# Normalised x, gated activations and most weights held as 16-bit parts in place of fp32r in a transformer block

## What is computed

```python
x = x + attn_a(layernorm(x), Wq, bq, Wk, bk, Wv, bv, Wo, bo)
x = x + ffn(layernorm(x), w_gate, w_up, w_down)
x = x + attn_b(layernorm(x), Wqkv, Wout, bout)
x = x + ffn(layernorm(x), w_gate, w_up, w_down)

def ffn(x, w_gate, w_up, w_down):          # integers of -127 to 127, times 1/127
    gate, up = x @ wg.T, x @ wu.T          # 256 -> 768
    return (silu(gate) * up) @ wd.T        # 768 -> 256
```

## Time and profile before

| | |
|---|---|
| Median of 3 runs | 2221.99 us (2216.15 to 2224.67) |
| Span of the profiled execution, and its own time | 2225.3 us |
| PE busy, share of the span | 1928.7 us, 87% |
| PE weight loads | 1388.2 us, 62% |
| DVE | 1422.0 us, 64% |
| ACT | 1444.9 us, 65% |
| POOL | 796.1 us, 36% |
| Matmuls traced | 25221 |

### The profile page before, as it was taken

How to read it: one execution, slowest core, us unless ns; L and a number is a source line. 1 busy time by engine, 2 the same in 40 slices (tenths; PEclk the granted TensorE clock), 3 DMA queues, 4 the chain that set the end, 5 groups by cost and what they waited for, 6 DMA issues and landing times.

```text
span 2225.3 us, 63347 instructions
## 1 busy us (share of the span) xinstructions
PE 1928.7 (87%) x25221; PEld 1388.2 (62%) x25221; DVE 1422.0 (64%) x2971; ACT 1444.9 (65%) x3580; POOL 796.1 (36%) x1131
## 2 busy tenths in 40 slices
PE   5677889889898989989898998989899898989786
PEld 4463657666675766667576666757666675756545
DVE  5363667576676757667675765767576676765624
ACT  1227676676867677676767767676776867677580
POOL 0023243433424343442434344243434424344431
PEclk7788999999999999999999999999999999999886
DMA  7224344252435335243533424353342434333321
GB/s 190 72 44 97 62 111 100 78 107 81 106 68 126 85 84 108 77 106 64 126 85 87 105 82 100 67 126 85 86 106 76 111 70 120 81 95 86 73 61 35
DMA packets 129636, 201.87 MB, mean 91 GB/s; under 512 B 26768, under 2 KB 60560, under 8 KB 129312
## 3 DMA queue, kind: packets, MB, share of 16 engines
q1 hardware_dynamic: 129344, 197.80, 37.1%
HBM read 67.87 MB, written 51.52 MB: 54 GB/s over the span
## 4 chain that ended last, share of the span: by engine, by line
PE 55%; ACT 17%; DVE 10%; issue 5%; SPq 5%; DMA 4%; POOL 4%; ACTq 0%; POOLq 0%; DVEq 0%
PE gu_bank L1053 15%; PE d_bank L1069 7%; ACT s_bank L1167 7%; PE gu_bank L1081 7%; SPq L575 4%; PE s_bank L984 4%; PE s_bank L948 4%; ACT probs_B L1157 3%; PE gu_bank L1017 3%; PE s_bank L814 2%; PE gu_bank L1027 2%; PE s_bank L969 2%; PE s_bank L822 2%; ACT probs_A L1150 2%; PE gu_bank L1004 2%
## 5 line engine op out<-in xcount | busy, mean ns | idle before, releaser
L1167 ACT ACTIVATE s_bank<-s_bank 128x512 f32<-128x512 f32 x1024 | 602.9, 591 | 123.3 <-PE s_bank L948 123.0
L1576 POOL TENSOR_TENSOR h<-tmp,h 128x512 fp32r<-128x512 f32 x192 | 252.0, 1312 | 451.6 <-DVE h L1457 451.6
L1157 ACT ACTIVATE probs_B<-s_bank 128x512 f32<-128x512 f32 x640 | 334.5, 610 | 48.5 <-PE s_bank L969 45.8
L1053 PE MATMUL gu_bank<-xT,w_g 128*128 128x256 f32 x1536 | 235.5, 298 | 25.1 <-DVE tmp L1440 21.1
L1053 PE MATMUL gu_bank<-xT,w_u 128*128 128x256 f32 x1536 | 241.3, 298 | 4.2 <-DVE tmp L1440 1.6
L1196 ACT ACTIVATE tmp<-gu_bank 128x512 f32<-128x512 f32 x192 | 114.6, 597 | 196.1 <-PE gu_bank L1053 188.5
L1053 PEld LDWEIGHTS gu_bank<-xT,w_g 128*128 128x128 f32 x1536 | 208.6, 199 | 52.9 <-DVE tmp L1440 35.8
L1053 PEld LDWEIGHTS gu_bank<-xT,w_u 128*128 128x128 f32 x1536 | 208.0, 198 | 37.6 <-issue 20.4
L1440 DVE SCALAR_TENSOR_TENSOR tmp<-tmp,gu_bank 128x512 f32<-128x512 f32 x192 | 130.6, 681 | 152.5 <-ACT tmp L1196 151.0
L1069 PE MATMUL d_bank<-w_d,h 128*128 128x256 f32 x1536 | 224.8, 288 | 3.3 <-POOL h L1576 3.3
L948 PE MATMUL s_bank<-pack_b 48*128 48x512 f16 x1024 | 180.4, 394 | 43.5 <-DVE o_raw L1361 19.9
(11 more groups left out here) (140 smaller groups left out, 3303.5 us busy)
## 6 DMA issues: line engine op xcount, KB each, us to landing
pack_b<-src_b SPq DMA_DIRECT2D x768, 64.0 KB, 2.6
pack_a<-src_a SPq DMA_DIRECT2D x384, 64.0 KB, 2.3
x<-in_L_attn_a_x_dram SPq DMA_DIRECT2D x32, 512.0 KB, 4.9
o_scr_A<-o_raw SPq DMA_DIRECT2D x64, 256.0 KB, 2.4
o_scr_B<-o_raw SPq DMA_DIRECT2D x64, 256.0 KB, 2.4
xn<-o_scr_A SPq DMA_DIRECT2D x32, 256.0 KB
rden_on<-r_scr_A SPq DMA_DIRECT2D x32, 256.0 KB
x_scr<-x SPq DMA_DIRECT2D x16, 512.0 KB, 2.9
```

Of the source, the lines that this page charges most:

```text
L1053: last = pe.matmul(bank[:, f * D:(f + 1) * D], plain(w[:, k, c:c + P], exact), plain(given[:, k, half * D:(half + 1) * D], exact), start=k ...
L1157: act.activation(probs["B"][:, i, :], score_bank("NP", n // 2, q, n % 2)[:, :], ACT.Exp, scale=SM_SCALE)\
L1167: act.activation(bank[:, :], bank[:, :], ACT.Exp, scale=SM_SCALE, accum_out=den[:, 0, j, 2 * tile + e, t:t + 1]).then_inc(den_exp, 1)
L1576: pool.tensor_tensor(h[1][:, i % 2, :], tmp[:, i % 2, :], h[0][:, i % 2, :].bitcast(F32), ALU.subtract)\
```

## The change

1. `xT`, `wa_qk`, `wa_v`, `wb_qk`, `wb_v` and `h` become f16, high and low part; `w_g`, `w_u` and `w_d` become bf16, of which the first of three tiles holds the whole integer. `wa_o`, `wb_o` and the attention's output stay fp32r, the latter in two tiles of its own, `on_part`.
2. So that small low parts stay in f16's range, the weights of queries, keys and values are multiplied by `W_SCALE = 16` when they are split (and the biases of attention A once on DVE); exp takes `SM_SCALE / W_SCALE ** 2`, and `wa_o`, `wb_o` are divided by 16. The gated activations are multiplied by `h_scale` (a per-partition scalar from the largest weight) and the result by `h_back`.
3. At the start ACT copies each bank of integer weights twice (bf16 tile and fp32 staging), the three DMAs of L554 go, and POOL splits the staged weights into three bf16 parts by nine instructions of 128x1536 after `GM` of the first sequence. Only `program(False)` reads the second and third part. `EXACT` falls from 2048 to 256; the weights here are at most 127.

The counts of PE's instructions in `program(True)` are what they were. The core of the diff:

```diff
-        wa_qk = [sb(f"wa_qk{i}", [P, KT, 2 * D], F32R) for i in range(2)]
+        wa_qk = [sb(f"wa_qk{i}", [P, KT, 2 * D], F16) for i in range(2)]
...
-        w_g = sb("w_g", [P, KT, HID], F32R)
+        w_g = [sb(f"w_g{i}", [P, KT, HID], BF16) for i in range(W_PARTS)]
...
-        xT = [[sb(f"xT{b}{i}", [P, KT, S], F32R) for i in range(2)] for b in range(2)]
+        xT = [[sb(f"xT{b}{i}", [P, KT, S], F16) for i in range(2)] for b in range(2)]
...
-        on_parts = xT[0]
+        on_parts = [sb(f"on_part{i}", [P, KT, S], F32R) for i in range(2)]
...
-        h = [sb(f"h{i}", [P, 2, S], F32R) for i in range(2)]
+        h = [sb(f"h{i}", [P, 2, S], F16) for i in range(2)]
...
-            for n, (dst, a) in enumerate(((w_g, st_gT), (w_u, st_uT), (w_d, st_dT))):
-                sp.wait_ge(w_staged, (4, 8, 11)[n])
-                sp.dma_start(dst[:, :, :].bitcast(F32), a).then_inc(w_raw, 16)
...
+                        for n, w_part in enumerate(w[:1] if exact else w):
+                            last = pe.matmul(bank[:, f * D:(f + 1) * D], w_part[:, k, c:c + P],
+                                             given[:, k, half * D:(half + 1) * D],
...
+                act.activation(dst[0], given, ACT.Copy)
+                act.activation(dst[1], given, ACT.Copy).then_inc(w_staged, 1)
-            act.wait_ge(w_raw, 48)
...
+            then(dve.tensor_scalar(h_back[:, :], w_top1, W_LEAST, 2.0, ALU.max, ALU.mult))
+            then(dve.tensor_tensor(h_back[:, :], h_back[:, :], h_back[:, :], ALU.mult))
+            then(dve.reciprocal(h_scale[:, :], h_back[:, :]))
+            then(dve.tensor_scalar(h_back[:, :], h_back[:, :], 0.5 * DEQUANT ** 3, None, ALU.mult))
...
-                dve.tensor_tensor(t, t, gu_of("U", i, block, q)[:, :], ALU.mult).then_inc(gu_taken, 1)
+                dve.scalar_tensor_tensor(t, t, h_scale[:, 0:1], gu_of("U", i, block, q)[:, :], ALU.mult, ALU.mult).then_inc(gu_taken, 1)
...
-                dve.scalar_tensor_tensor(xs, tokens(d_bank), 0.5 * DEQUANT ** 3, xs, ALU.mult, ALU.add).then_inc(d_taken, 1)
+                dve.scalar_tensor_tensor(xs, tokens(d_bank), h_back[:, 0:1], xs, ALU.mult, ALU.add).then_inc(d_taken, 1)
...
+                    if q == 0:
+                        split_weights()
```

More of the change, by code:

```diff
@@ L411, in build @@
         wb_split = sem("wb_split")
-        w_raw = sem("w_raw")
+        w_parts = sem("w_parts")
+        b_scaled = sem("b_scaled")
+        w_spread = sem("w_spread")
         w_flag = sem("w_flag")
@@ L1047, in ffn_up @@
                     gu("GU"[up], i, block, q)
+                if not exact and part == 0 and i == 0 and FN[block, q] == 0:
+                    pe.wait_ge(w_parts, 3 * W_PARTS)
                 for k in range(KT):
@@ L1052, in ffn_up @@
                         c = (2 * pair + f) * P
-                        last = pe.matmul(bank[:, f * D:(f + 1) * D], plain(w[:, k, c:c + P], exact),
-                                         plain(given[:, k, half * D:(half + 1) * D], exact),
-                                         start=k == 0 and part == 0 and f == 0, stop=k == KT - 1 and part == 1, skip_group_check=True)
+                        for n, w_part in enumerate(w[:1] if exact else w):
+                            last = pe.matmul(bank[:, f * D:(f + 1) * D], w_part[:, k, c:c + P],
+                                             given[:, k, half * D:(half + 1) * D],
+                                             start=k == 0 and part == 0 and f == 0 and n == 0, stop=k == KT - 1 and part == 1,
+                                             skip_group_check=True)
                 if part:
@@ L1068, in ffn_down @@
                             c = f * D + t * P
-                            last = pe.matmul(bank[:, t, :], plain(h[part][:, i % 2, c:c + P], exact), plain(w_d[:, 2 * pair + f, :], exact),
-                                             start=pair == 0 and f == 0 and part == 0 and t == 0,
-                                             stop=pair == FT // 2 - 1 and f == 1 and part == 1, skip_group_check=True)
+                            for n, w_part in enumerate(w_d[:1] if exact else w_d):
+                                last = pe.matmul(bank[:, t, :], h[part][:, i % 2, c:c + P], w_part[:, 2 * pair + f, :],
+                                                 start=pair == 0 and f == 0 and part == 0 and t == 0 and n == 0,
+                                                 stop=pair == FT // 2 - 1 and f == 1 and part == 1, skip_group_check=True)
                 last.then_inc(d_ready if pair == FT // 2 - 1 else h_used, 1)
@@ L1265, in then, with split @@
                 dve.wait_ge(prep, done[0])
-            def split(parts, a):
-                then(dve.tensor_copy(parts[0], a))
-                return dve.tensor_tensor(parts[1], a, parts[0].bitcast(F32), ALU.subtract)
+            def split(parts, a, scale):
+                then(dve.tensor_scalar(parts[0], a, scale, None, ALU.mult))
+                high = parts[0].bitcast(F32) if scale < 1 else parts[0]
+                return dve.scalar_tensor_tensor(parts[1], a, scale, high, ALU.mult, ALU.subtract)
             def split_bank(n):
@@ L1275, in split_bank @@
                 w, c = ((wa_qk, 0), (wa_qk, D), (wa_v, 0), (wa_o, 0))[n]
-                split([a[:, :, c:c + D] for a in w], bank).then_inc(w_taken, 1)
+                split([a[:, :, c:c + D] for a in w], bank, W_SCALE if n < 3 else 1.0 / W_SCALE).then_inc(w_taken, 1)
             def to_float(n):
@@ L1609, in global_blocks, with split_weights @@
                     .then_inc(blocks_ready, 1)
+            def split_weights():
+                pool.wait_ge(w_staged, NBANKS - NSPLIT)
+                staged = (st_gT, st_uT, st_dT)
+                for n, (parts, rest) in enumerate(zip((w_g, w_u, w_d), staged)):
+                    pool.tensor_tensor(rest, rest, parts[0][:, :, :], ALU.subtract).then_inc(w_parts, 1)
+                    pool.wait_ge(w_parts, n * W_PARTS + 1)
+                    pool.tensor_copy(parts[1][:, :, :], rest).then_inc(w_parts, 1)
+                    pool.wait_ge(w_parts, n * W_PARTS + 2)
+                    pool.tensor_tensor(parts[2][:, :, :], rest, parts[1][:, :, :], ALU.subtract).then_inc(w_parts, 1)
             def global_maxima(q):
```

65 lines of the change are left out of this document (38 added, 27 removed).

## The result

The changed kernel takes 2150.1 us (median of four runs, 2146.4 to 2153.6) against 2219.1 us of the kernel before in the same series: a ratio of 0.9686, 95% interval 0.9665 to 0.9707. It is 69 us faster; 2168 were predicted, with a range of 2118 to 2207. The profiled execution of after has a span of 2151.9 us, 73.4 less than the 2225.3 of before. In the code after, L1053 has become L1057, L1069 L1075, L1081 L1087, L1004 L1008, L1017 L1021, L1027 L1031, L1446 L1466, L1457 L1477, L1462 L1482 and L1576 L1596.

The account below looks back on a forecast made before the run. PE was taken as the bound in most of a turn, ACT and DVE in a smaller part. From the profiled 2225.3 us, -61 + 3 + 4 = -54 gave 2171, then 2168 as the median is 3.3 lower; range 2118 to 2207.

Parts of the forecast that it names:

- Part 1: Matmul steps within groups on PE: f16 shortens them, saving 3.4 us (256 columns) and 1.0 us (512) a turn.
- Part 2: First matmul of PE groups whose weight load is exposed: 0.11 us falls to 0.01, taken as 2.0 us a turn.
- How much arrives: Share of PE's saving that reaches the end: 70%, 4.2 us a turn, 61 us over 14.6 turns.
- the first rival: ACT's exp and DVE's emptying of PSUM banks set the pace, a third of PE's gain arrives: 2198 us; chance 0.15.
- The clock: Rival: with PE in flight for less of each turn, further stretches fall to 1.2 GHz: 2243 us; chance 0.07.
- Theory C: Posed with the experiments: less time at the lower granted clock makes the gain, not the matmuls' steps; no chance given.
- DVE: Per-partition scalars add 1.0 us of DVE a turn, a sixth counts: 0.2 us a turn, 2 to 3 in all.
- The start: Second staging copies, tiny DVE instructions and POOL's split delay the start once: +4 us (2 to 9).
- The first 230 us and the end: First 230 and last 96 us: few sequences to interleave, then latency; no gain counted there.
- others take over: ACT and DVE limit once PE is quicker, a third of PE's gain arrives: 2198 us; chance 0.15.
- All arrives: Rival: every term at its upper bound and all on the path: 2120 us; chance 0.12.
- no quick load: Rival: weight loads stay at 0.11 us in bf16 beside f16, only costs remain: 2229 us; chance 0.06.

Follow-up runs that it names:

- rates: The kernel after with rows of 17 matmuls behind its last one; fp32r with 256 columns took 0.118 us a step with 128x128 and 128x32 weights, f16 0.109.
- The doses: First matmul of 24 gate and up groups a turn run two more times, in the kernel after (2201.5 us) and in the kernel before (2293.2 us).
- after_again: The kernel after, unchanged, run once more as a base on the same chip: 2152.6 us, ratio 0.9680 to before.
- before_pe_dose: The kernel before with the first matmul of 24 gate and up groups a turn run two more times: 2293.2 us, ratio 1.0325.
- pool_dose: The kernel after with a 128x4 memset before each of POOL's h_low steps, 12 times a turn: 2154.9 us, ratio 0.9709.
- out_f16: The kernel after with the output projections in f16 too and the factor 1/256 in the addition to x: 2145.0 us, ratio 0.9661.

## Why the prediction was right, and where it was not

**Part 1, steps within a group: size right, reason wrong.** 0.119 to 0.109 us and 0.236 to 0.215 were the forecast; the earlier trace rows and the rows of after give 0.119 to 0.109, and the starts in the trace 0.234 to 0.216 for 512 columns. The numbers came from rows of the same shapes, so they hold. The reason, "the two together come to 0.119", was wrong: `rates` keeps the step with a quarter of the weight columns. The 512-column row could have told: its streaming (0.213) hides a load of 0.11 entirely, and it had the larger excess (0.236).

**Part 2, first matmul of a group: right.** 0.11 us exposed for fp32r, 0.01 for f16: a fresh group of eight went from 1.22 to 1.05, of which 0.07 are its seven steps and 0.10 its start. Over all groups at the full clock, the first step of L1053 went from a mean of 0.170 to 0.114 us, of L1069 from 0.176 to 0.114, of L1004 from 0.187 to 0.112 and of L1081 from 0.286 to 0.224. For both parts together, take for each matmul at the full clock the time to the next start, or its own where none follows before it ends: the means went from 0.131 to 0.117 us (L1053), 0.133 to 0.117 (L1069), 0.132 to 0.117 (L1004) and 0.253 to 0.230 (L1081). That is 192 x 0.014 + 96 x 0.016 + 48 x 0.014 + 48 x 0.023 = 6.0 us a turn, where the sum had 6.4.

**How much arrives: right.** 70% was taken between 88% from the chain and the 35% of the first rival. The doses measured 0.79 and 0.58 at the two ends, 0.69 between, each uncertain by 0.08. 14.6 turns x 6.0 x 0.69 = 60 us, where 61 were predicted.

**The clock: the sign was missed.** It stood in the prediction as a risk only, and at the measured place it went the other way. The long stretch of steady turns, before and then after:

```profile
230.00:2000.00 1770.00, 1598.66 (x21708) 1154.05 (x21704) 1199.45 (x2520) 1227.45 (x3042) 676.90 (x952) 0.97 0.39 93
```

```profile
230.00:2000.00 1770.00, 1560.24 (x22195) 972.28 (x22193) 1241.44 (x2589) 1267.67 (x3172) 680.99 (x993) 0.98 0.38 96
```

The granted clock is 0.98 instead of 0.97 although PE is busy for less of the time. Summed from the trace's record of it, the time at the lower level in this stretch is 113 us before, 55 after and 61 in after_again; over the whole span 272, 190 and 217. More work on PE lowers it too: 79 in this stretch of before_pe_dose. Before, such stretches recur about each turn, at 1096.8, 1229.9 and 1356.2 us among others, the first one the four matmuls of 1.05 us in the earlier trace rows; between 1195 and 1800 us there are nine of them, none in after and three in after_again.

PE's time shows it as well. The four changed lines took 945 us before and 825 after, 120 less. Of these, 16 x 6.0 = 96 are steps at the full clock; the other 24 go with fewer of their matmuls at the lower level, 152 instead of 357. All other lines took 7.5 us more, which leaves the 112.7 less of PE's busy time.

What the clock is worth can be read from the runs, whose mean clock is on record: a run at a mean clock of 0.94 has 2 x 0.06 of its time at the lower level. The 25 runs of before beside the experiments have 0.944 on average, 250 us at the lower level, the nine of after 0.954, 199 us: 51 less, where the two traces have 82, since the traced run of before had one of the lower clocks (0.939). Among the 25 runs of one and the same kernel, the time rises by 0.24 us for each us more at the lower level (0.16 among the nine of after). If it is the clock that makes those runs longer, and not something that also lowers the clock, it gave 8 to 12 us of the gain, an estimate from these runs. Turns of the two traces give more: the two of before with the least of the lower level take 128.1 us each, the six of after with as much 124.6 on average, 3.5 apart, where all turns are 5.0 apart; 1.5 a turn, some 19 us over thirteen, is then left for the clock, but these are few turns. Theory C is thus a small part of the gain. No run isolates it, and why the clock falls less often, no run here shows.

**DVE: the duration was right, the weight too low.** L1466 took 0.746 us and L1482 0.747 (0.750 expected), the cast to f16 0.455: it kept the fast rate, as taken. But the 15 us that these two lines are busy longer count by 0.30 to 0.56, not a sixth: 5 to 8 us instead of 3. (DVE's busy time as a whole rose by 7 us only, 1422.0 to 1429.2; what it lost elsewhere no run prices.) The step that failed is "DVE is 10% of the chain for 64% of busy time, so a sixth".

**POOL: right within what was measured.** `h_low` went to 1.186 us (1.165 expected), and pool_dose can't tell whether that was worth 0 or 6 us.

**The start: right in its parts, smaller in the end.** First normalisation at 25.7 us (25 expected), PE 2.2 us later. Of this 1.1 us are left at the first FFN's addition to x (143.8 against 142.7), where the first saved steps are in it already. The casts of the split took 1.46 us and the two-input steps 3.09, where 1.9 and 3.9 were taken; it ended at 90.4 and not near 93, and cost nothing. 4 us were charged, 1 was left at that point.

**The first 230 us and the end: not nothing.** By the last addition behind the first FFN, the 73.4 us between the two traces lie as follows: 4.9 us up to the second sequence's (278.3 against 273.4), 64.4 in the thirteen turns behind it, and 4.1 from the fifteenth's to the end (268.4 against 264.3; 259.8 in after_again, so 4 to 9). Outside these thirteen turns, then, some 9 us were gained, although the start costs something; there the prediction had the remaining 1.6 of its 14.6 turns, 6 us, less 4 for the start. Steps and fresh starts are shorter there too wherever the clock is full. A steady turn gained 5.0 us (64.4 over thirteen), where 4.0 were predicted (4.2 less 0.2 for DVE).

**The sum:** 96 x 0.69 = 66 from the steps of all sixteen sequences, about 10 from the clock, less 7 for DVE and 1 for the start, is 68 us, and 69 were measured; the prediction had 61 - 3 - 4 = 54. The uncertainty of the shares alone is 8 us here, so the close agreement is partly luck. The steps that failed are three, each small: the clock was counted as a danger and not as a gain (about 10 us), the stretches outside the steady turns as nothing (5 us of steps), and the charge for the start was too high by 3; the low weight of DVE, 4 us, went the other way.

Of the rivals, *others take over* began to come true: PE stands 39 us longer in all, in the long stretch 14.7 instead of 12.5 us a turn, 2.2 more and under the 3 that were named (3.7 more in the one turn shown above), and its wait for DVE's gate step has grown (us in total, times, longest; before, then after):

```profile
PE gu_bank L1053 <- DVE tmp L1440: 22.7, 22, 1.6
```

```profile
PE gu_bank L1057 <- DVE tmp L1460: 33.5, 28, 3.0
```

It did not get to its 35%: the lower of the two shares measured is 0.58, at the least 0.49. *All arrives* and *no quick load* are excluded, the latter by 0.11 us of fresh start that went to 0.01.

## What to carry to other kernels

A row of equal matmuls is priced by a row of the same shape and type in the trace, not by adding up its causes: the price held here where the cause was wrong. For fp32r against f16 with 256 or more moving columns, count 8 to 10% of the streaming time, as measured here, and 0.07 to 0.1 us for each group whose first weight load is exposed; of the widths measured only 128 and 64 columns are bound by the load.

The share of PE's time that reaches the end falls as PE gets faster (0.79, then 0.58; the 5 us for the 17 that PE is busy less in out_f16 are too uncertain to add to this), so a gain is priced with the mean of the shares at both ends, and the next one with the lower. A dose of known length, put at one engine in the kernel before and in the one after, measures both in two runs. It did better here than the engine's part of one chain, but it moves the clock as well, so the granted clock of the dosed runs has to be read beside it.
